# Second chunk's first ternary ahead of the minimum over the lags, and both row sums behind the next group's first copy, in an octonion FFN kernel with a lag bound

## The chip, the cores and the metric

The kernel runs on one core of a Trainium2 chip. The metric is device time in microseconds; three runs of the kernel before gave 606.47, 607.83 and 608.39, so the median is 607.83. A core has a matrix engine, TensorE (PE in the profile, its weight loads PEld), and three engines for elementwise work: VectorE (DVE), ScalarE (ACT) and GpSimd (POOL). SyncE (SP) issues the DMAs. Each engine takes its instructions in the order in which they are written and waits on semaphores that the others raise; an instruction that waits holds up everything behind it on its engine.

## The reference

The input x has 2048 rows of 1024 values. Each row is normalised, and two branches are added to x: an attention over time lags, and a feed-forward net whose weights are ternary and multiplied as octonions.

```python
x = L0_attn_x
xn = _layernorm(x, axis=-1)
x = x + _L0_attn_ref(xn) + _L0_ffn_ref(xn, w_gate, w_up, w_down)

# attention: circular autocorrelation by FFT, softmax over the 6 largest lags, weighted sum of rolled rows
f = jnp.fft.rfft(xh, axis=-1)
corr = jnp.fft.irfft(f * jnp.conj(f), n=L, axis=-1)
weights, delay = jax.lax.top_k(corr, top_k)

# feed-forward: every weight tensor W (8, out/8, in/8) is made ternary with one threshold
scale = jnp.mean(jnp.abs(W))
Wq = scale * jnp.clip(jnp.round(W / scale), -1.0, 1.0)
M = jnp.einsum('jik,jod->koid', S_OCT, Wq)      # S_OCT: the signed table of octonion products
out = jnp.einsum('...id,koid->...ko', xp, M)
# h = silu(gate(x)) * up(x), then down(h);  w_gate, w_up: (8, 341, 128), w_down: (8, 128, 341)
```

For these inputs the lag at zero dominates the softmax so far that the attention branch is the normalised row itself. The kernel proves that row by row with a bound (it needs the smallest value over the lags of a short transform) and only takes a slow path where the bound fails.

## The kernel before

The 2048 rows are taken in 8 groups of 256 rows, each of two tiles of 128. The 341 hidden values of each octonion part are split into three chunks c of 114, 114 and 113. The work is a list of units, and each unit owns one of four pairs of accumulator banks, `acc`:

- T(m,c): transposes of the weights of matrix m (0 gate, 1 up, 2 down), chunk c. ACT then takes signs (L636), DVE turns them ternary in place of the sign (`ternary`, L906), and DVE builds sums and differences of weight blocks from them (`weight_slots`, L923 to L931).
- X(g,i): transposes of half of the normalised x of group g (L419), split by ACT and DVE in a high and a low 16-bit part.
- G(g,c,Y) and U(g,c,Y): gate and up products of chunk c, output half Y. After the spectral part (L375) ACT copies two of the four quarters to `pk` (`odd_two`, L681), DVE adds and subtracts (`first_adds` L980 to L984, `second_adds` L1014 to L1028), and PE adds the terms (L382). For G, ACT applies SiLU (L707 to L710); for U, DVE multiplies into `hx` (`product`, L1077). In group 0 the first two chunks are computed directly (L402).
- For each product, POOL forms half sums (L1313 to L1319), and ACT and POOL round the product (ACT L725, POOL L1321) and the sums (ACT L736, POOL L1324) into the 16-bit operand `hop` of the down product.
- N(g,t): the down product of one tile (L479), scaled and added to the output tile by DVE (L1172).
- F(g): a transform of the folded x (L432), its power by ACT (L695), and the lag matmuls (L440). DVE then takes the minimum over the lags (`least`, L1082).

The layer norm of group g is made while group g-1 runs: ACT sums each of the two tiles (`row_sum`, L585, and the mean at L588), then their squares (`row_var`, L599); POOL makes 1/sqrt by one power and one Newton step (`rstd`, L1270 to L1283), ACT normalises (L604), and DVE multiplies the halves of each row (`dot`, L939). After that the unit X of group g can be transposed.

What comes after what is written out. The opening (weights and group 0) is a list for each engine. The steady part is one loop over the places n of the unit list, in which every engine has its own dictionaries of what to add at which place. PE makes the spectral part of unit n and then the terms of unit n-2. A group begins with G(b,0,0), U(b,0,0), and the unit ahead of it is F(b). Before a unit begins, PE waits until the unit that owned its banks before has been read (`take_banks`).

Of the kernel before, what the change touches and what calls it, by code (L numbers as in the profile page):

```python
def octonion_ffn_attention_kernel(nc, x, w_gate, w_up, w_down, dft, lag, out):
# [15 lines left out]
    G = ROWS // T  # L17
# [70 lines left out]
    place = {u: n for n, u in enumerate(units)}  # L88
# [36 lines left out]
    sum_at, var_at, rstd_at, norm_at, dot_at = {}, {}, {}, {}, {}  # L125
    for g in range(2, G):
        a, b = g - 2, g - 1
        sum_at[place["F", b]], sum_at[place["G", b, 0, 0]] = (g, 0), (g, 1)
        var_at[place["U", b, 0, 0]], var_at[place["G", b, 0, 1]] = (g, 0), (g, 1)
        rstd_at[u_no["U", b, 0, 0]] = g  # L130
        norm_at[place["N", b - 1, 0]] = g
# [14 lines left out]
    for u in u_no:  # L146
        _, g, c, Y = u
# [11 lines left out]
    with ctx:  # L159
# [414 lines left out]
        def _(act):  # L574
# [5 lines left out]
            def row_sum(g, t):  # L580
                k = NT * g + t
                act.wait_ge(x_in[t], 16 * (g + 1))
                act.wait_ge(sum_done, k - 1)
                act.wait_ge(var_done, NT * g)
                nc.scalar.activation(junk[:, :], xr[:, t, :], ACT.Copy, accum_out=sm[:, k:k + 1]).then_inc(sum_done, 1)  # L585
                if t == NT - 1:
                    act.wait_ge(sum_done, k)
                    nc.scalar.activation(nm[:, NT * g:NT * g + NT], sm[:, NT * g:NT * g + NT], ACT.Copy, scale=-1.0 / D).then_inc(mean_done, 1)  # L588
# [12 lines left out]
            def normalise(g, t):  # L601
                k = NT * g + t
                act.wait_ge(ln_done, g + 1)
                nc.scalar.activation(xr[:, t, :], xr[:, t, :], ACT.Identity, bias=nmrs[:, k:k + 1], scale=rs[:, k:k + 1]).then_inc(norm_done, 1)  # L604
# [78 lines left out]
            def x_high(u):  # L683
                act.wait_ge(x_mm, x_no[u] + 1)
                nc.scalar.activation(xop[:, u[1] % 2, 4 * u[2]:4 * u[2] + 4, 0, :], bank_pair(place[u]).rearrange("p b (i t) -> p (b i) t", t=T),
                                     ACT.Copy, scale=XS).then_inc(xhi_done, 1)
# [6 lines left out]
            def power(u):  # L693
                act.wait_ge(dft_mm, f_no[u] + 1)
                nc.scalar.activation(pw[:, :, :].rearrange("p m t -> p (m t)"), acc[:, bank[place[u]], 0, :], ACT.Square, scale=POWER).then_inc(power_done, 1)  # L695
# [16 lines left out]
            def h_high(u):  # L712
                _, g, c, Y = u
                m = u_no[u]
                h = hx[0:CH, m % 4, :, :]
                if m == 0:
                    act.wait_ge(abs_done[2], 1)
                if m < LAST:
                    act.wait_ge(h_done, m + 1)
                else:  # L720
                    act.wait_ge(tail_pair, 2)
                    h = last_h
                for v in free_after[g, c]:
                    act.wait_ge(term_mm, prod_no[v] + 1)
                nc.scalar.activation(half_of(g, c, 4 * Y, 0), by_tile(h), ACT.Copy).then_inc(hhi_done, 1)  # L725

            def h_sums_high(u):
                _, g, c, Y = u
                m = u_no[u]
                if m < LAST:  # L730
                    act.wait_ge(hs_done, 2 * m + 2)
                    sums = hs[:, 0:4, :]
                else:
                    act.wait_ge(tail_sum, 2)
                    sums = last_sums
                nc.scalar.activation(half_of(g, c, NJ + 4 * Y, 0), by_tile(sums), ACT.Copy).then_inc(hhs_done if m < LAST else tail_high, 1)  # L736
# [64 lines left out]
            for n in range(OPEN, N + 8):  # L801
                if n in norm_at:
                    normalise(norm_at[n], 0)
                    normalise(norm_at[n], 1)
                if n in z_at:
                    g, t = z_at[n]
                    k = NT * g + t
                    act.wait_ge(zx_in[t], 16 * (g + 1))
                    nc.scalar.activation(zx[:, t, :], zx[:, t, :], ACT.Identity, bias=nmrs[:, k:k + 1], scale=onep[:, k:k + 1]).then_inc(z_done, 1)
                if n in round_at:  # L810
                    h_sums_high(round_at[n])
                if n in high_at:
                    h_high(high_at[n])
                if 2 <= n < N and units[n - 2] == ("U", G - 1, NC - 1, 1):

                    for b in range(2):
                        act.wait_ge(tail_mult, b + 1)
                        nc.scalar.activation(hx[0:CH, LAST % 4, 2 * b + 1, :], last_h[:, 2 * b + 1, :], ACT.Copy).then_inc(tail_odd, 1)
                if n < N:
                    u = units[n]  # L820
                    if u[0] in "GUNX":
                        odd_two(u)
                    if u[0] == "X":
                        x_high(u)
                    if u[0] == "F":
                        power(u)
                if n in x_sums:
                    x_sums_high(x_sums[n])
                if n in silu_at:
                    silu(silu_at[n])  # L830
                if n == OPEN + 1:
                    eights(("T", 1, 1))
                if n in sum_at:
                    row_sum(*sum_at[n])
                if n in var_at:
                    row_var(*var_at[n])

# [18 lines left out]
        def _(dve):  # L856
# [43 lines left out]
            def ternary(u):  # L900
                _, m, c = u
                k, n = t_no[u], place[u]
                rows, cols, val = weights_of(u)
                for b in range(2):
                    dve.wait_ge(sign_done, 2 * k + b + 1)
                    nc.vector.scalar_tensor_tensor(val[:, 4 * b:4 * b + 4, :],  # L906
                                                   acc[0:rows, bank[n], b, :].rearrange("p (j d) -> p j d", j=4)[:, :, 0:cols],
                                                   thr[0:rows, m:m + 1], wt[k % 2][0:rows, 4 * b:4 * b + 4, 0:cols], ALU.is_gt, ALU.min).then_inc(tern_done, 1)

            def weight_slots(u):  # L910
                _, m, c = u
                i = slots_no[u]
                rows, cols, val = weights_of(u)
                dve.wait_ge(tern_done, 2 * t_no[u] + 2)
                two = val.rearrange("p (b i v) d -> p b i v d", b=2, i=2)
                s = tt[i % 2][0:rows, :, :, 0:cols]
                if u == ("T", 1, 0):

                    dve.wait_ge(first_slots, 1)
                if u == ("T", 2, 2):  # L920

                    dve.wait_ge(term_mm, prod_no["G", 0, 1, 1] + 1)
                nc.vector.tensor_tensor(s[:, 0:3:2, :, :], two[:, :, 0, :, :], two[:, :, 1, :, :], ALU.add)  # L923
                nc.vector.tensor_tensor(s[:, 1:4:2, :, :], two[:, :, 0, :, :], two[:, :, 1, :, :], ALU.subtract).then_inc(pairs_done, 1)
                dve.wait_ge(pairs_done, i + 1)
                for op, (a, alu) in enumerate(((0, ALU.add), (0, ALU.subtract), (1, ALU.add), (1, ALU.subtract))):
                    if m < 2:
                        dst = (wg, wu)[m][:, c, 4 * op:4 * op + 4, 0:cols].rearrange("p (b v) d -> p b v d", b=2)
                    else:
                        dst = wd[0:rows, 4 * op:4 * op + 4, c, :].rearrange("p (b v) d -> p b v d", b=2)  # L930
                    last = nc.vector.tensor_tensor(dst, s[:, a:a + 1, :, :].broadcast_to([rows, 2, 2, cols]), s[:, 2:4, :, :], alu)  # L931
                last.then_inc(slots_done, 1)
# [147 lines left out]
            def least(u):  # L1080
                dve.wait_ge(lag_mm, f_no[u] + 1)
                nc.vector.tensor_reduce(dmin[:, NT * u[1]:NT * u[1] + NT], acc[:, bank[place[u]], 1, :].rearrange("p (t l) -> p t l", t=NT),  # L1082
                                        AX.X, ALU.min).then_inc(bound_done, 1)
# [30 lines left out]
            weight_slots(("T", 1, 2))  # L1114

            product(("U", 0, 0, 0))
            least(("F", 0))
            ternary(("T", 0, 1))
            weight_slots(("T", 0, 1))
            ternary(("T", 1, 1))  # L1120
            thresholds(2, ("T", 1, 1))
            product(("U", 0, 0, 1))
# [20 lines left out]
            for n in range(OPEN, N + 2):  # L1143
# [19 lines left out]
                if n >= OPEN + 2:  # L1163
                    v = units[n - 2]
                    if v[0] == "N":
                        _, g, t = v
# [193 lines left out]
```

## Time and profile before

| | before |
|---|---|
| median of 3 runs | 607.83 us (606.47 to 608.39) |
| the profiled execution, time | 607.72 us |
| the profiled execution, span | 605.7 us |
| PE busy | 583.6 us, 96% |
| weight loads (PEld) | 543.0 us, 90% |
| DVE busy | 508.4 us, 84% |
| POOL busy | 462.8 us, 76% |
| ACT busy | 354.7 us, 59% |

The span is that of one profiled execution, and its own time lies 2.0 us above it. PE's matmuls overlap and their ends are modelled, so 96% busy doesn't mean that the array is never kept waiting for a weight load; but the gaps that the profile does show are short and few. Busy shares of the other engines say little by themselves: what counts is which of them PE waits for at a given place.

### The profile page before, as it was taken

The numbers are of one execution on the slowest core, as the hardware profiler recorded it, in microseconds if no ns is written. First come the engines' busy times: TensorE is split into PE (matmuls) and PEld (weight loads), VectorE is DVE, ScalarE is ACT, GpSimd is POOL, SyncE is SP. The second block draws the span as 40 slices with busy tenths as digits, with TensorE's granted clock in tenths as the row PEclk, the third lists the DMA queues.
The fourth block names the chain that finished last, engine by engine and source line by source line (L and its number), as shares of the span: only waits on it lengthen the run. The fifth ranks groups of instructions, "written<-read, shape, count | busy, mean of one in ns | idle before, by whom it ended". The sixth has DMA issues, their size and how long they took to land.

```text
span 605.7 us, 16440 instructions
## 1 busy us (share of the span) xinstructions
PE 583.6 (96%) x6764; PEld 543.0 (90%) x6764; DVE 508.4 (84%) x1230; ACT 354.7 (59%) x497; POOL 462.8 (76%) x362
## 2 busy tenths in 40 slices
PE   7998999979999999999999999999999999999996
PEld 7998998869989998899989998899989998998896
DVE  4886898879898989989888989989898989967854
ACT  4677967664567635774476545774576645543540
POOL 3415749998769977999769977999679977987920
PEclk9999999999999999999999999999999999999999
DMA  9720011001040023002040013002030101002011
GB/s 208 158 71 1 1 71 71 2 1 70 3 140 2 4 71 119 22 2 70 3 140 2 37 37 141 1 2 72 1 140 2 42 32 70 2 3 70 1 71 72
DMA packets 10251, 30.67 MB, mean 51 GB/s; under 512 B 928, under 2 KB 4032, under 8 KB 10176
## 3 DMA queue, kind: packets, MB, share of 16 engines
q1 hardware_dynamic: 10176, 29.62, 15.3%
q8 instruction: 53, 0.87, 0.6%
q14 instruction: 22, 0.18, 0.1%
HBM read 21.23 MB, written 8.39 MB: 49 GB/s over the span
## 4 chain that ended last, share of the span: by engine, by line
POOL 54%; issue 30%; PE 14%; DVE 1%; POOLq 0%; ACT 0%; ACTq 0%
POOL hop L1324 16%; POOL hs L1318 10%; POOL hs L1319 10%; POOL hs L1314 9%; POOL hs L1313 6%; PE acc L479 5%; PE acc L402 4%; PE acc L411 2%; PE acc L382 1%; POOL r L1272 1%; POOL hop L1321 1%; PE acc L456 1%; PE acc L375 0%; POOL hop L1254 0%; PE acc L419 0%
## 5 line engine op out<-in xcount | busy, mean ns | idle before, releaser
L479 PE MATMUL acc<-wd,hop 114*128 114x128 f16 (+1 forms) x2944 | 171.4, 220 | 1.0 <-POOL hop L1324 0.7
L479 PEld LDWEIGHTS acc<-wd,hop 114*128 114x128 f16 (+1 forms) x2944 | 168.3, 98 | 2.2 <-POOL hop L1324 0.9
L681 ACT ACTIVATE pk<-acc 114x512 f32<-114x512 f32 (+1 forms) x120 | 70.7, 589 | 71.6 <-PE acc L479 34.1
L1313 POOL TENSOR_TENSOR hs<-hx 114x512 f32<-114x512 f32 x47 | 60.3, 1282 | 68.4 <-DVE hx L1077 60.4
L1324 POOL TENSOR_TENSOR hop<-hs,hop 114x1024 f16<-114x1024 f32 x46 | 98.2, 2135 | 7.9 <-ACT hop L736 7.9
L1321 POOL TENSOR_TENSOR hop<-hx,hop 114x1024 f16<-114x1024 f32 x46 | 98.3, 2138 | 0.6 <-ACT hop L725 0.6
L382 PE MATMUL acc<-xop,wg 128*128 128x256 f16 x704 | 84.1, 273 | 4.5 <-DVE acc L1028 4.4
L725 ACT ACTIVATE hop<-hx 114x1024 f16<-114x1024 f32 x46 | 48.6, 1057 | 65.4 <-DVE hx L1077 65.4
L375 PE MATMUL acc<-xop,wg 128*128 128x256 f16 x704 | 84.2, 273 | 1.0 <-DVE hx L1077 0.9
L382 PE MATMUL acc<-xop,wu 128*128 128x256 f16 x704 | 84.1, 273 | 0.7
L375 PE MATMUL acc<-xop,wu 128*128 128x256 f16 x704 | 84.1, 273 | 0.7 <-DVE hx L1077 0.7
L980 DVE TENSOR_TENSOR bd<-acc,pk 114x256 f32<-114x256 f32 (+1 forms) x104 | 43.7, 421 | 48.2 <-ACT pk L681 48.0
L382 PEld LDWEIGHTS acc<-xop,wg 128*128 128x128 f16 x704 | 68.3, 98 | 14.2 <-DVE acc L1028 6.0
L375 PEld LDWEIGHTS acc<-xop,wu 128*128 128x128 f16 x704 | 68.7, 98 | 9.2 <-DVE hx L1077 1.0
L375 PEld LDWEIGHTS acc<-xop,wg 128*128 128x128 f16 x704 | 67.7, 98 | 10.2 <-DVE hx L1077 2.6
L382 PEld LDWEIGHTS acc<-xop,wu 128*128 128x128 f16 x704 | 67.8, 98 | 10.0 <-DVE acc L1028 2.3
L736 ACT ACTIVATE hop<-hs 114x1024 f16<-114x1024 f32 x46 | 48.6, 1057 | 45.6 <-POOL hs L1319 45.4
L1318 POOL TENSOR_TENSOR hs<-hs 114x512 f32<-114x512 f32 x47 | 62.4, 1328 | 3.7
L1319 POOL TENSOR_TENSOR hs<-hs 114x512 f32<-114x512 f32 x47 | 62.5, 1331 | 0.0
L1077 DVE SCALAR_TENSOR_TENSOR hx<-hx,few,acc 114x1024 f32<-114x1024 f32 x47 | 59.8, 1272 | 1.8 <-PE acc L402 1.8
L1314 POOL TENSOR_TENSOR hs<-hx 114x512 f32<-114x512 f32 x47 | 60.2, 1280 | 0.0
L984 DVE TENSOR_TENSOR acc<-acc,pk 114x256 f32<-114x256 f32 (+1 forms) x104 | 44.0, 423 | 0.0
(164 smaller groups left out, 929.3 us busy)
## 6 DMA issues: line engine op xcount, KB each, us to landing
xr<-in_x SPq DMA_DIRECT2D x16, 512.0 KB, 4.8
zx<-in_x SPq DMA_DIRECT2D x16, 512.0 KB, 4.0
out_y<-zx SPq DMA_DIRECT2D x16, 512.0 KB, 3.0
hop<-in_w_down SPq DMA_DIRECT2D x1, 1364.0 KB, 19.3
hop<-in_w_gate SPq DMA_DIRECT2D x2, 576.0 KB, 9.5
hop<-in_w_up SPq DMA_DIRECT2D x1, 1152.0 KB
hop<-in_w_gate SPq DMA_DIRECT2D x1, 192.0 KB
hop<-in_w_up SPq DMA_DIRECT2D x1, 192.0 KB
```

Source lines behind the costliest of these rows:

```text
L375: last = nc.tensor.matmul(acc[:, bank[n], s // 2, T * (s % 2):T * (s % 2 + 1)], wm[:, c, slot, :], xop[:, g % 2, form, level, :], start=s ...
L382: last = nc.tensor.matmul(acc[:, bank[n], s // 2, T * (s % 2):T * (s % 2 + 1)], wm[:, c, slot, :], xop[:, g % 2, form, level, :], start=Fa ...
L479: last = nc.tensor.matmul(acc[:, bank[n], s // 2, at:at + P], operand(g, c, t, form, level), wd[0:WIDE[c], slot, c, :], start=which == 0 a ...
L681: nc.scalar.activation(pk[0:rows, q % 2, :, :], pair[:, :, T:2 * T], ACT.Copy, scale=XS if u[0] == "X" else 1.0).then_inc(copied, 1)
L725: nc.scalar.activation(half_of(g, c, 4 * Y, 0), by_tile(h), ACT.Copy).then_inc(hhi_done, 1)
L1077: nc.vector.scalar_tensor_tensor(hx[0:CH, m % 4, :, :], hx[0:CH, m % 4, :, :], scale[0:CH, :], bank_pair(place[u], CH).rearrange("p b (i t ...
L1313: nc.gpsimd.tensor_tensor(hs[:, 4:8:2, :], h[:, 0:4:2, :], h[:, 1:4:2, :], ALU.add)
L1314: nc.gpsimd.tensor_tensor(hs[:, 5:8:2, :], h[:, 0:4:2, :], h[:, 1:4:2, :], ALU.subtract).then_inc(hpair_done, 1)
L1318: nc.gpsimd.tensor_tensor(hs[:, 0:2, :], hs[:, 4:6, :], hs[:, 6:8, :], ALU.add).then_inc(hs_done, 1)
L1319: nc.gpsimd.tensor_tensor(hs[:, 2:4, :], hs[:, 4:6, :], hs[:, 6:8, :], ALU.subtract).then_inc(hs_done, 1)
L1321: nc.gpsimd.tensor_tensor(half_of(g, c, 4 * Y, 1), by_tile(h), half_of(g, c, 4 * Y, 0), ALU.subtract).then_inc(h_free, 1)
L1324: nc.gpsimd.tensor_tensor(half_of(g, c, NJ + 4 * Y, 1), by_tile(hs[:, 0:4, :]), half_of(g, c, NJ + 4 * Y, 0), ALU.subtract).then_inc(h_rea ...
```

## The change

Two places are written in another order; no instruction is added or removed.

```diff
-        sum_at[place["F", b]], sum_at[place["G", b, 0, 0]] = (g, 0), (g, 1)
+        sum_at[place["G", b, 0, 0]] = g
...
                 if n in sum_at:
-                    row_sum(*sum_at[n])
+                    row_sum(sum_at[n], 0)
+                    row_sum(sum_at[n], 1)
...
             product(("U", 0, 0, 0))
-            least(("F", 0))
             ternary(("T", 0, 1))
             weight_slots(("T", 0, 1))
+            least(("F", 0))
             ternary(("T", 1, 1))
```

The code after is one line longer ahead of VectorE's part, so its lines there have numbers higher by one (L906 becomes L907, L1324 becomes L1325); ScalarE's keep theirs up to L834.

VectorE, opening, before: the product of U(0,0,0) (L1077), the minimum over the lags of F(0) (L1082, `dmin`), the ternary of T(0,1) (L906 on `wg`), its sums (L923 to L931), and the ternary of T(1,1) (L906 on `wu`).

```order
L1077 SCALAR_TENSOR_TENSOR hx<-hx,few,acc 114x1024
L1082 TENSOR_REDUCE dmin<-acc 128x2
L906 SCALAR_TENSOR_TENSOR wg<-acc,few,zx 128x4x114 x2
L923 TENSOR_TENSOR zx<-wg 128x2x2x114
L924 TENSOR_TENSOR zx<-wg 128x2x2x114
L931 TENSOR_TENSOR wg<-zx 128x4x114 x4
L906 SCALAR_TENSOR_TENSOR wu<-acc,few,zx 128x4x114 x2
```

VectorE, the same place, after the change (line numbers one higher).

```order
L1078 SCALAR_TENSOR_TENSOR hx<-hx,few,acc 114x1024
L907 SCALAR_TENSOR_TENSOR wg<-acc,few,zx 128x4x114 x2
L924 TENSOR_TENSOR zx<-wg 128x2x2x114
L925 TENSOR_TENSOR zx<-wg 128x2x2x114
L932 TENSOR_TENSOR wg<-zx 128x4x114 x4
L1083 TENSOR_REDUCE dmin<-acc 128x2
L907 SCALAR_TENSOR_TENSOR wu<-acc,few,zx 128x4x114 x2
```

The minimum has moved behind eight instructions, the ternary of T(0,1) and its sums; nothing else on VectorE differs.

ScalarE at the start of group 2, before: the power of F(2) (L695), SiLU of the last gate unit of group 1 (L710), a row sum, the copy of G(2,0,0) to `pk` (L681), the other row sum and the mean, and then rounding of the half sums (L736) and of the product (L725).

```order
L695 ACTIVATE pw<-acc 128x512 [waits dft_mm]
L710 ACTIVATE hx<-acc,few 114x1024 [waits h_free,term_mm]
L585 ACTIVATE junk,sm<-xr 128x1024 [waits var_done,sum_done,x_in0]
L681 ACTIVATE pk<-acc 114x512 [waits spec_mm,l1_done]
L585 ACTIVATE junk,sm<-xr 128x1024 [waits var_done,sum_done,x_in1]
L588 ACTIVATE nm<-sm 128x2 [waits sum_done]
L736 ACTIVATE hop<-hs 114x2x4x128 [waits hs_done]
L725 ACTIVATE hop<-hx 114x2x4x128 [waits term_mm,h_done]
```

ScalarE, the same place, after the change.

```order
L695 ACTIVATE pw<-acc 128x512 [waits dft_mm]
L710 ACTIVATE hx<-acc,few 114x1024 [waits h_free,term_mm]
L681 ACTIVATE pk<-acc 114x512 [waits spec_mm,l1_done]
L585 ACTIVATE junk,sm<-xr 128x1024 [waits var_done,sum_done,x_in0]
L585 ACTIVATE junk,sm<-xr 128x1024 [waits var_done,sum_done,x_in1]
L588 ACTIVATE nm<-sm 128x2 [waits sum_done]
L736 ACTIVATE hop<-hs 114x2x4x128 [waits hs_done]
L725 ACTIVATE hop<-hx 114x2x4x128 [waits term_mm,h_done]
```

The copy has moved ahead of the first row sum, and the two row sums now stand one behind the other. The same happens at the start of groups 1 to 6; group 1 differs in that L725 alone stands behind the mean, and the rounding of the sums follows later. Queues of TensorE, GpSimd and SyncE are the same as before.

## Rows read from the trace of the kernel before

**Rows 1.** The waits of TensorE (PE): us in total, times, longest us.
```profile
PE acc L382 <- DVE acc L1028: 4.4, 6, 0.7
...
PE acc L419 <- DVE hx L1077: 2.8, 1, 2.8
```

**Rows 2.** Timeline, PE, opening: start us, duration us, instruction [idle before <-releaser].
```profile
47.98 0.60 PE L440 MATMUL acc<-lag_sb,pw 128*128 128x256 f16 x4
50.56 1.00 PE L456 MATMUL acc<-ident,hop 114*128 114x114 f32 x8 [1.98 <-DVE wg L906]
...
55.07 1.04 PE L419 MATMUL acc<-ident,xr 128*128 128x128 f32 x8
...
59.44 1.04 PE L456 MATMUL acc<-ident,hop 128*114 128x128 f32 x8
```

**Rows 3.** Timeline, VectorE (DVE), same place.
```profile
48.62 0.69 DVE L1082 TENSOR_REDUCE dmin<-acc 128x2 f32<-128x512 f32 x1 [3.87 <-PE acc L440]
49.23 1.28 DVE L906 SCALAR_TENSOR_TENSOR wg<-acc,few,zx 128x456 f16<-128x456 f32 x2
```

**Rows 4.** Timeline, ScalarE (ACT), opening.
```profile
37.76 1.06 ACT L585 ACTIVATE junk<-xr 128x1024 f16<-128x1024 f32 x1
...
38.99 1.06 ACT L585 ACTIVATE junk<-xr 128x1024 f16<-128x1024 f32 x1
...
44.69 1.17 ACT L636 ACTIVATE zx<-acc,few 128x456 f16<-128x456 f32 x2 [0.19 <-PE acc L456]
...
48.21 2.36 ACT L604 ACTIVATE xr<-xr,nmrs,rs 128x1024 f32<-128x1024 f32 x2
```

**Rows 5.** Timeline, ACT, first pair of row sums moved (start of group 1).
```profile
103.41 1.06 ACT L585 ACTIVATE junk<-xr 128x1024 f16<-128x1024 f32 x1
...
104.45 0.59 ACT L681 ACTIVATE pk<-acc 114x512 f32<-114x512 f32 x1
```

**Rows 6.** Timeline, DVE, same place.
```profile
106.41 1.27 DVE L1077 SCALAR_TENSOR_TENSOR hx<-hx,few,acc 114x1024 f32<-114x1024 f32 x1
```

**Rows 7.** Timeline, PE, group 1.
```profile
107.74 1.92 PE L375 MATMUL acc<-xop,wg 128*128 128x256 f16 x16 [0.89 <-DVE hx L1077]
...
122.84 1.96 PE L479 MATMUL acc<-wd,hop 113*128 113x128 f16 x32 [0.74 <-POOL hop L1324]
...
134.14 7.16 PE L479 MATMUL acc<-wd,hop 114*128 114x128 f16 x96 [0.24 <-DVE acc L1002]
```

**Rows 8.** Timeline, GpSimd (POOL), group 1.
```profile
111.41 2.14 POOL L1324 TENSOR_TENSOR hop<-hs,hop 114x1024 f16<-114x1024 f32 x1 [0.54 <-ACT hop L736]
```

**Rows 9.** Timeline, ACT, group 2.
```profile
177.44 0.58 ACT L681 ACTIVATE pk<-acc 114x512 f32<-114x512 f32 x1
177.92 1.05 ACT L585 ACTIVATE junk<-xr 128x1024 f16<-128x1024 f32 x1
...
179.20 1.04 ACT L736 ACTIVATE hop<-hs 114x1024 f16<-114x1024 f32 x1
...
194.34 2.37 ACT L604 ACTIVATE xr<-xr,nmrs,rs 128x1024 f32<-128x1024 f32 x2 [0.98 <-POOL onep L1283]
```

**Rows 10.** Timeline, POOL, group 2.
```profile
180.32 2.13 POOL L1324 TENSOR_TENSOR hop<-hs,hop 114x1024 f16<-114x1024 f32 x1 [1.03 <-ACT hop L736]
```

**Rows 11.** Timeline, DVE, group 2.
```profile
200.38 1.27 DVE L1077 SCALAR_TENSOR_TENSOR hx<-hx,few,acc 114x1024 f32<-114x1024 f32 x1
...
202.56 0.42 DVE L1002 TENSOR_TENSOR acc<-acc,bd 128x256 f32<-128x256 f32 x1
```

**Rows 12.** Timeline, PE, group 2.
```profile
175.19 1.91 PE L375 MATMUL acc<-xop,wg 128*128 128x256 f16 x16
...
202.24 1.04 PE L419 MATMUL acc<-ident,xr 128*128 128x128 f32 x8
203.11 5.53 PE L479 MATMUL acc<-wd,hop 114*128 114x128 f16 x96
```

**Rows 13.** Windows: stretch, us, busy of PE, PEld, DVE, ACT, POOL; granted clock; DMA.
```profile
134.00:136.00 2.00, 1.86 (x20) 1.86 (x21) 1.73 (x6) 2.00 (x5) 2.00 (x2) 0.60 0.00 0
```

## The prediction, written before the changed kernel was run

> **What bounds the kernel now.** I read the list of TensorE's waits first, because TensorE (PE) has almost no idle time: the reader is to see that only a few short waits are left, and that every one is ended by an instruction of DVE or POOL [rows 1]. The largest family, six waits of 0.7 us behind DVE L1028, lies at the end of each group, before the row sums start; it is a loop of PE, ACT and DVE over the last unit of the group, and the change moves nothing in it. Two others belong to the change: the wait of 1.98 us behind DVE L906 at 50.56 in the opening [rows 2], and 0.89 us behind DVE L1077 at 107.74 [rows 7]. Next I read the timeline of each engine round those two places, and last round the same place one group later, since the row sums come back six times (g from 2 to 7, beside groups 1 to 6) and a wait that is absent today may appear there. Groups 2 to 6 repeat one pattern, so rows of group 2 stand for five.
>
> **The opening.** Today DVE reaches the minimum over the lags early and stands for 3.87 us until the lag matmuls are done; only then come the two instructions of the ternary T(0,1), at 49.23 for 1.28 us [rows 3]. PE, which finished those lag matmuls at 48.58, needs the bank of T(0,1) for the transposes of T(1,1) and waits 1.98 us, until 50.56 [rows 2]. The signs that the ternary needs are ready at 44.69 + 1.17 = 45.86 [rows 4]. With the ternary first, its second half can start at about 45.9 and be done at 46.6, which is 2 us before PE asks for the bank. So the wait goes, and nothing on DVE takes its place: the sums of T(0,1) (6 instructions) fill the time in which DVE stood idle, and the minimum starts about when it does today. Since ends of overlapping matmuls are modelled (four take 0.60, but PE issues one every (1.91 - 0.27)/15 = 0.11 us by a row of 16 [rows 12], taking 0.27 for one), PE could go on as early as 47.98 + 0.44 = 48.42. That bounds the gain by 1.98 and 2.14 us; I take 2.1.
>
> What is late next? The normalisation on ACT ends at 48.21 + 2.36 = 50.57 [rows 4]; its reader, the transposes of X(1,0), stands at 55.07 [rows 2] and would stand at 53.0. The signs of T(1,1) follow the normalisation at 50.5, their ternary is done by 52.5, and their bank is asked for by T(2,0) at 59.44 today [rows 2], 57.3 then. POOL starts its first product earlier, but it later stands waiting for a DVE product anyway, so that buys nothing and costs nothing. From there to the end of the opening PE is busy without a wait, and what feeds it is fed by it, so I let the 2.1 us through in full.
>
> **Row sums, group 1.** The first sum now stands between SiLU and the copy `pk`: it starts at 103.41, the copy at 104.45 [rows 5]. With the copy first, DVE's quad and then its product come 1.04 us earlier than 106.41 [rows 6], and PE's unit at 107.74, which waits for that product's end at 107.68 (so a released engine starts 0.06 us later), comes at 106.7: the 0.89 us are gone [rows 7]. But the next wait is POOL's: PE stands 0.74 us at 122.84 for POOL's last rounding [rows 7], and POOL was held up only 0.54 us by ACT [rows 8]. ACT is ahead there by 1.04, so POOL gains those 0.54 and no more. PE arrives a full 1.04 earlier and waits longer. Gain of this group: 0.55 us.
>
> **Row sums, groups 2 to 6.** Here PE's spectral unit ends at 175.19 + 1.91 = 177.10 [rows 12], and the copy starts at 177.44, just behind the first row sum. So the copy can gain at most about 0.25 us (177.2 instead of 177.44). The price is on ACT behind it. Today the first sum fits into the time in which ACT would wait for PE. Then it follows the copy: first sum at 177.2 + 0.48 (the step from the copy to the next instruction today, [rows 9]) = 177.68. Two row sums in a row are also not 1.04 apart but 38.99 - 37.76 = 1.23 us [rows 4], because the second waits for the first one's accumulator to be read: second sum at 178.91. Today it starts at 177.92, and the rounding of the half sums, L736, at 179.20 [rows 9], 1.28 later. So L736 moves to 180.19, later by 0.99 us. This is the queue behind the moved instruction, and POOL waits for its head: POOL L1324 already waits 1.03 us for exactly L736 [rows 10].
>
> From there I follow the 1.0 us. POOL works through that unit, the next one and then the Newton steps of the layer norm, with no idle between; ACT's normalisation at 194.34 has waited 0.98 us for POOL, so it follows in full [rows 9]. DVE's two dots wait for the normalisation; behind them on DVE's queue stand the quad of the unit N, the product at 200.38 and the second sums, whose last ends at 202.56 + 0.42 = 202.98 [rows 11]. PE needs these at 202.24 (transposes; the product ends at 201.65, slack 0.59 less the 0.06) and at 203.11 (terms of N; slack 0.13 less 0.06 = 0.07) [rows 12]. Slack 0.07 against a delay of 0.99: PE loses 0.92 us in each such group. Up to 1.0 is possible if a later unit leans on the same DVE queue without slack. The delay is not given back before the group ends, since there PE sets the pace; and POOL's backlog is gone by then, so the five do not pile up. Five times 0.92 to 1.0 is 4.6 to 5.0; I take 4.8. Below: were the pair 1.04 apart, the delay would be 0.80 and the sum 5 x 0.73 = 3.7; were DVE to find a way round, nothing.
>
> **Sum.** -2.1 - 0.55 + 4.8 = +2.15 us on the profiled execution's 607.72, so 609.9. Its own time is 0.1 us below the median of the runs shown (607.83), so I leave it there.
>
> **A place where the clock speaks.** TensorE was idle 2.76 us before the transposes of group 1 (the 2.8 of [rows 1]); behind that, the granted clock averages 0.60 over 134 to 136 us, a mix of 2.4 and 1.2 GHz [rows 13], and 96 matmuls take 7.16 instead of 5.53 us [rows 7, 12], a loss of 1.63. The Trainium skill, page "TensorE: Matmul & The Clock Gate", section "Why this matters for your kernels", warns that idle gaps between bursts bring TensorE back to half rate. By that rule the trace agrees, and it speaks for the same loss after, because the 2.76 us behind POOL's chain stay: the order of the products there is unchanged.
>
> **Rivals.**
> (a) *The delay never reaches PE.* If DVE or ACT has more slack than I read, only the gains stand: 607.72 - 2.65 = 605.1, faster by 0.4%. For it: POOL and ACT are far from full over the span and wait in other places. Against: 0.98 and 1.03 us of idle on the chain itself, both ended by its predecessor, say that the chain is tight. Chance 0.15.
> (b) *Only part of it comes through*, 0.3 to 0.7 us a group (the second sum does not wait 1.23, or the product's earlier start shifts DVE's queue): 606.6 to 608.6, middle 607.9. Chance 0.18.
> (c) *The opening gives nothing*: PE's 2.1 us turn into a wait at X(1,0) or at the end of the opening, while groups 2 to 6 cost 4.8: 612.0, slower. For it: ACT and DVE are dense up to 90 us; against: PE is never idle between 51 and 106 us and both queues hang on PE. Chance 0.10.
> (d) *The clock.* The slow stretch does not come, 608.3, or comes a second time since PE's idle in group 1 is 0.5 us longer in sum, 611.5. Chance 0.07, half each.
> My forecast has 0.50. A kernel of this length is told from no change at about 0.3%, 1.8 us. Faster is (a), 0.15. Within 0.3% are (b), half of (d) and a quarter of the forecast's own spread: 0.18 + 0.03 + 0.12 = 0.33. Slower is the rest, 0.52. The forecast's own range is 608.8 to 611.0; the one that holds 8 in 10 reaches from 606.2 to 612.1.
>
> **What would show it.** In the opening: no PE wait behind DVE L907 (L906 moved by one line), DVE's minimum behind the sums. Group 1: the 0.89 gone, the wait for POOL grown from 0.74 to about 1.2. Groups 2 to 6: ACT's rounding about 1.0 later behind the copy, POOL L1325 waiting 2.0 instead of 1.0, and new PE waits at the transposes of X (0.4) and at N's terms (0.5) that add up to 0.9 five times, with each of these groups longer by that. If their length stays, (a) holds and I am wrong in sign; if the two PE waits are there but small, (b).

## The result, and the profile after

| | before | after |
|---|---|---|
| median | 608.19 us (9 runs, 606.47 to 609.35) | 609.78 us (9 runs, 608.79 to 610.44) |
| ratio | | 1.0037, 95% interval 1.0027 to 1.0047 |
| the profiled execution, time and span | 607.72 and 605.7 us | 609.15 and 607.1 us |
| PE busy | 583.6 us | 585.6 us |
| POOL busy | 462.8 us | 462.9 us |

The changed kernel is slower by 0.37%, about 2.2 us by the ratio. The forecast was 609.9 us, with slower as the likeliest outcome.

TensorE's waits in the profile after (us in total, times, longest):

```profile
PE acc L382 <- DVE acc L1029: 4.4, 6, 0.7
...
PE acc L419 <- DVE hx L1078: 3.2, 4, 2.8
PE acc L479 <- DVE acc L1003: 1.2, 5, 0.2
PE acc L479 <- POOL hop L1325: 1.2, 1, 1.2
```

The wait behind the ternary (DVE L906 before, L907 now) has left the list. In its stead the transposes of X wait four times instead of once, the terms of N five times instead of once, and the wait for POOL has grown from 0.74 to 1.18 us. The six waits of 0.7 at the ends of groups are the ones of [rows 1].

The opening, TensorE and then VectorE (columns as in [rows 2]):

```profile
47.81 0.60 PE L440 MATMUL acc<-lag_sb,pw 128*128 128x256 f16 x4
48.25 0.94 PE L456 MATMUL acc<-ident,hop 114*128 114x114 f32 x8
```

```profile
45.19 1.29 DVE L907 SCALAR_TENSOR_TENSOR wg<-acc,few,zx 128x456 f16<-128x456 f32 x2 [0.61 <-ACT zx L636]
...
48.49 0.68 DVE L1083 TENSOR_REDUCE dmin<-acc 128x2 f32<-128x512 f32 x1
```

The transposes of T(1,1) follow the lag matmuls at once, 0.44 us after their start, where they came 2.58 us after it in [rows 2]. The ternary of T(0,1) is over at 46.5, and the minimum starts at 48.49, which in [rows 3] was 48.62: VectorE's idle time really was filled.

Group 1, TensorE and POOL:

```profile
104.34 1.92 PE L375 MATMUL acc<-xop,wg 128*128 128x256 f16 x16
...
119.88 1.96 PE L479 MATMUL acc<-wd,hop 113*128 113x128 f16 x32 [1.18 <-POOL hop L1325]
...
129.83 1.93 PE L419 MATMUL acc<-ident,xr 128*128 128x128 f32 x8 [2.75 <-DVE hx L1078]
131.56 6.37 PE L479 MATMUL acc<-wd,hop 114*128 114x128 f16 x96
```

```profile
108.47 2.13 POOL L1325 TENSOR_TENSOR hop<-hs,hop 114x1024 f16<-114x1024 f32 x1
```

The wait of 0.89 us at G(1,0,1) ([rows 7]) is gone, and POOL L1325 no longer waits for ScalarE as it did in [rows 8]. TensorE now stands longer for POOL at 119.88, and then as long as before, 2.75 us, at the transposes of X. The slow stretch of the clock is here again, in another place: it covers the transposes (1.93 us for 8) and part of the terms of N (6.37 us for 96, where it was 7.16 in [rows 7]).

Group 2, ScalarE, POOL, VectorE and TensorE, the rows that answer to [rows 9 to 12]:

```profile
173.81 0.60 ACT L681 ACTIVATE pk<-acc 114x512 f32<-114x512 f32 x1 [0.69 <-PE acc L375]
174.31 1.05 ACT L585 ACTIVATE junk<-xr 128x1024 f16<-128x1024 f32 x1
...
175.53 1.06 ACT L585 ACTIVATE junk<-xr 128x1024 f16<-128x1024 f32 x1
...
176.82 1.04 ACT L736 ACTIVATE hop<-hs 114x1024 f16<-114x1024 f32 x1
...
191.95 2.37 ACT L604 ACTIVATE xr<-xr,nmrs,rs 128x1024 f32<-128x1024 f32 x2 [1.55 <-POOL onep L1284]
```

```profile
177.94 2.13 POOL L1325 TENSOR_TENSOR hop<-hs,hop 114x1024 f16<-114x1024 f32 x1 [2.02 <-ACT hop L736]
```

```profile
197.99 1.26 DVE L1078 SCALAR_TENSOR_TENSOR hx<-hx,few,acc 114x1024 f32<-114x1024 f32 x1
```

```profile
170.05 1.92 PE L382 MATMUL acc<-xop,wg 128*128 128x256 f16 x16 [0.72 <-DVE acc L1029]
...
199.31 1.09 PE L419 MATMUL acc<-ident,xr 128*128 128x128 f32 x8
200.65 5.53 PE L479 MATMUL acc<-wd,hop 114*128 114x128 f16 x96 [0.25 <-DVE acc L1003]
...
238.34 1.92 PE L382 MATMUL acc<-xop,wg 128*128 128x256 f16 x16 [0.72 <-DVE acc L1029]
...
511.53 1.92 PE L382 MATMUL acc<-xop,wg 128*128 128x256 f16 x16 [0.73 <-DVE acc L1029]
```

The rows of the kernel before that are counted from, at X's transposes of group 1 and at the first terms of groups 2 and 7:

```profile
132.80 1.09 PE L419 MATMUL acc<-ident,xr 128*128 128x128 f32 x8 [2.76 <-DVE hx L1077]
...
173.43 1.92 PE L382 MATMUL acc<-xop,wg 128*128 128x256 f16 x16 [0.73 <-DVE acc L1028]
...
510.09 1.92 PE L382 MATMUL acc<-xop,wg 128*128 128x256 f16 x16 [0.73 <-DVE acc L1028]
```

To compare with before, count from the start of the group's first terms, L382, at 173.43 before and 170.05 after. The rounding L736 came 5.77 us behind it and now comes 6.77; POOL L1324/L1325 6.89 and 7.89; the normalisation 20.91 and 21.90; VectorE's product 26.95 and 27.94; the transposes of X 28.81 and 29.26; N's terms 29.68 and 30.60. So ScalarE's 1.0 us arrives at VectorE whole, and 0.92 of it at TensorE. From group to group TensorE's L382 is 68.29 us apart (238.34 - 170.05); before, the mean of the five periods from 173.43 to 510.09 is 67.33. This distance is called the period below. Five such groups are 4.8 us.

### The profile page after: what moved, and what is told of

It is laid out like the page before. It is cut to its first block, busy times and chain, and to the rows that moved or that the text cites. A ratio compares the mean times of both kernels' runs of the same rounds, so it can differ in the third digit from the quotient of the medians.

```text
span 607.1 us, 16440 instructions
## 1 busy us (share of the span) xinstructions
PE 585.6 (96%) x6764; PEld 541.6 (89%) x6764; DVE 508.3 (84%) x1230; ACT 354.9 (58%) x497; POOL 462.9 (76%) x362
## 4 chain that ended last, share of the span: by engine, by line
POOL 53%; issue 31%; PE 11%; DMA 2%; DVE 1%; SPq 0%; ACT 0%; POOLq 0%; ACTq 0%
POOL hop L1325 15%; POOL hs L1319 10%; POOL hs L1320 10%; POOL hs L1315 9%; POOL hs L1314 6%; PE acc L479 5%; PE acc L402 4%; DMA hop<-in_w_gate 2%; PE acc L382 1%; POOL r L1273 1%; POOL hop L1322 1%; PE acc L456 1%; PE acc L375 0%; PE acc L419 0%; PE acc L411 0%
## 5 line engine op out<-in xcount | busy, mean ns | idle before, releaser
L681 ACT ACTIVATE pk<-acc 114x512 f32<-114x512 f32 (+1 forms) x120 | 70.5, 588 | 71.2 <-PE acc L375 37.1
L1325 POOL TENSOR_TENSOR hop<-hs,hop 114x1024 f16<-114x1024 f32 x46 | 98.1, 2133 | 12.8 <-ACT hop L736 12.8
L382 PE MATMUL acc<-xop,wg 128*128 128x256 f16 x704 | 84.1, 273 | 4.5 <-DVE acc L1029 4.4
L382 PE MATMUL acc<-xop,wu 128*128 128x256 f16 x704 | 84.1, 273 | 0.7
L725 ACT ACTIVATE hop<-hx 114x1024 f16<-114x1024 f32 x46 | 48.5, 1055 | 59.4 <-DVE hx L1078 59.4
L382 PEld LDWEIGHTS acc<-xop,wg 128*128 128x128 f16 x704 | 68.3, 98 | 14.2 <-DVE acc L1029 6.0
L736 ACT ACTIVATE hop<-hs 114x1024 f16<-114x1024 f32 x46 | 48.6, 1056 | 53.1 <-POOL hs L1320 53.1
L382 PEld LDWEIGHTS acc<-xop,wu 128*128 128x128 f16 x704 | 67.8, 98 | 9.9 <-DVE acc L1029 2.4
```

Of the source, the lines that this page charges most:

```text
L382: last = nc.tensor.matmul(acc[:, bank[n], s // 2, T * (s % 2):T * (s % 2 + 1)], wm[:, c, slot, :], xop[:, g % 2, form, level, :], start=Fa ...
L681: nc.scalar.activation(pk[0:rows, q % 2, :, :], pair[:, :, T:2 * T], ACT.Copy, scale=XS if u[0] == "X" else 1.0).then_inc(copied, 1)
L1325: nc.gpsimd.tensor_tensor(half_of(g, c, NJ + 4 * Y, 1), by_tile(hs[:, 0:4, :]), half_of(g, c, NJ + 4 * Y, 0), ALU.subtract).then_inc(h_rea ...
```

## The experiments

All ran beside runs of the kernel before (median 607.73 us beside the first four, 607.71 beside the last three). Each was written to move one term of the sum or to cut the chain at one place.

**Opening only.** VectorE's order in the opening is changed, ScalarE's is that of before.

```diff
-            least(("F", 0))
             ternary(("T", 0, 1))
             weight_slots(("T", 0, 1))
+            least(("F", 0))
```

> Only the opening's reorder on VectorE (ternary and sums of T(0,1) ahead of the minimum), row sums as before. My theory: the three terms are independent, so this one alone takes 2.1 us off: ratio 0.9965, about 606.1 against 608.2, and TensorE's wait behind the ternary at 50.6 is gone while every later wait of before (0.89, 0.74, 2.76, six of 0.73) is still there. Rival A, the opening's gain is given back later in the opening or at POOL's wait in group 1: ratio 1.000. Rival B, the opening is where the change loses: above 1.002.

Measured: 604.88 us, ratio 0.9951 (0.9939 to 0.9964). TensorE:

```profile
48.38 0.94 PE L456 MATMUL acc<-ident,hop 114*128 114x114 f32 x8
...
105.51 1.92 PE L375 MATMUL acc<-xop,wg 128*128 128x256 f16 x16 [0.89 <-DVE hx L1077]
...
120.59 1.96 PE L479 MATMUL acc<-wd,hop 113*128 113x128 f16 x32 [0.73 <-POOL hop L1324]
...
130.55 1.69 PE L419 MATMUL acc<-ident,xr 128*128 128x128 f32 x8 [2.76 <-DVE hx L1077]
```

The waits of 0.89, 0.74 and 2.76 us are still there, so the gain is the opening's and is passed on whole: T(1,1) starts 2.18 us earlier than in [rows 2], the unit behind the 0.89 us 2.23 us earlier than in [rows 7]. Rivals A and B fall. The timed gain, 2.85 us by the medians, is 0.7 larger than I had expected; 0.4 of it, in the profiled execution, is the slow stretch, which in this profile starts at the transposes and in the one of before in N's terms (from X's transposes to the next group's L382 are 40.22 us here, 40.63 in the profile of before). The rest is within the interval.

**Row sums only.** The opening is that of before, the row sums are those of the changed kernel.

```diff
-        sum_at[place["F", b]], sum_at[place["G", b, 0, 0]] = (g, 0), (g, 1)
+        sum_at[place["G", b, 0, 0]] = g
```

> Only the row sums' reorder on ScalarE, opening as before. My theory: -0.6 in group 1 and +0.96 in each of groups 2 to 6, +4.2 in all: ratio 1.0070, about 612.4. TensorE's new waits stand at the transposes of X and the terms of N, and the rounding L736 comes 1.0 later. Rival: the reorder is neutral by itself and only costs together with the opening (ratio 1.000); or the loss is in one place only (ratio 1.000 to 1.003).

Measured: 612.02 us, ratio 1.0075 (1.006 to 1.009). TensorE's waits:

```profile
PE acc L419 <- DVE hx L1078: 3.6, 6, 2.8
...
PE acc L456 <- DVE wg L907: 2.0, 1, 2.0
PE acc L479 <- DVE acc L1003: 1.5, 6, 0.2
```

The opening's wait is back, and the waits at X and N are there, six of each where the changed kernel has four and five. The period is 68.32 us, as in the changed kernel. The profiled execution took 611.0 us, 1.0 less than the median: it has no slow stretch of the clock, and the six runs spread from 610.7 to 613.4. The two halves of the change add up: 0.9951 x 1.0075 = 1.0026, with the interval of the whole (1.0027 to 1.0047) inside what the intervals of the two allow. The rival that the halves need one another falls.

**Row sums moved in group 1 only**, with the opening's reorder.

```diff
+        if g == 2:
+            sum_at[place["G", b, 0, 0]] = ((g, 0), (g, 1))
+        else:
+            sum_at[place["F", b]], sum_at[place["G", b, 0, 0]] = ((g, 0),), ((g, 1),)
```

> Opening's reorder, and the row sums moved behind the copy only at the start of group 1; groups 2 to 6 as before. My theory: -2.1 and -0.6 without the cost: ratio 0.9955, about 605.5, faster than both kernels. In groups 2 to 6 the pattern of before comes back: L736 waited for 1.03 us by POOL, period 67.33. Rival, the loss of the changed kernel came from group 1 or from the phase in which the groups start: the period stays at 68.3 and the ratio is 1.002 or more.

Measured: 604.65 us, ratio 0.9950 (0.9938 to 0.9962): faster than both kernels. POOL and TensorE in group 2:

```profile
176.95 2.13 POOL L1328 TENSOR_TENSOR hop<-hs,hop 114x1024 f16<-114x1024 f32 x1 [1.03 <-ACT hop L739]
```

```profile
170.05 1.92 PE L385 MATMUL acc<-xop,wg 128*128 128x256 f16 x16 [0.72 <-DVE acc L1032]
...
237.39 1.92 PE L385 MATMUL acc<-xop,wg 128*128 128x256 f16 x16 [0.73 <-DVE acc L1032]
```

TensorE at X's transposes of group 1:

```profile
129.78 1.39 PE L422 MATMUL acc<-ident,xr 128*128 128x128 f32 x8 [2.77 <-DVE hx L1081]
```

POOL waits 1.03 us for the rounding, as before, and the group takes 67.34 us: the loss was in groups 2 to 6, and not in the phase that the opening hands on. What the move is worth in group 1 the times can't tell (604.65 against 604.88, each uncertain by 0.7). The traces show it: X's transposes start 0.77 us earlier than in the kernel with the opening alone (129.78 and 130.55). In this kernel the opening's T(1,1) already starts 0.22 us earlier (48.16 and 48.38), so the move in group 1 is worth 0.55 us.

**The dots taken off the chain.** The changed kernel, with VectorE's two dots one unit N later.

```diff
+        dot_at[place["N", b - 1, 1]] = g
...
-                if n in norm_at and kind == "N":
-                    dot(norm_at[n], 0)
-                    dot(norm_at[n], 1)
+                if n in dot_at:
+                    dot(dot_at[n], 0)
+                    dot(dot_at[n], 1)
```

> The changed kernel with one thing more: VectorE's two dots of the normalised rows (L939) no longer stand ahead of the quad of N(b-1,0) but ahead of that of N(b-1,1), where VectorE idles 2 us. They are what ties the product and N's sums to POOL's Newton steps and ScalarE's normalisation. My theory: ScalarE's rounding is still 1.0 late and POOL still waits 2.0 for it, but it reaches TensorE no more: the 0.96 us of each of groups 2 to 6 vanish (-4.8), and the 2.76 us of idle in group 1 shrinks to about 1 (-1.8): ratio to before about 0.992, 603.2. Rival, the delay reaches TensorE by another way (POOL's rounding of the operands for N, or the banks): the period stays near 68.3 and only group 1 gains, ratio about 1.000.

Measured: 603.26 us, ratio 0.9927 (0.9915 to 0.9939). POOL and TensorE:

```profile
175.73 2.13 POOL L1326 TENSOR_TENSOR hop<-hs,hop 114x1024 f16<-114x1024 f32 x1 [2.03 <-ACT hop L737]
```

```profile
127.90 1.09 PE L420 MATMUL acc<-ident,xr 128*128 128x128 f32 x8 [0.94 <-DVE hx L1079]
...
167.84 1.92 PE L383 MATMUL acc<-xop,wg 128*128 128x256 f16 x16 [0.73 <-DVE acc L1030]
...
177.31 1.91 PE L383 MATMUL acc<-xop,wg 128*128 128x256 f16 x16
179.18 1.92 PE L376 MATMUL acc<-xop,wu 128*128 128x256 f16 x16
...
235.31 1.92 PE L383 MATMUL acc<-xop,wg 128*128 128x256 f16 x16 [0.72 <-DVE acc L1030]
```

This is the sharpest of the tests: POOL still waits 2.03 us for the late rounding, exactly as in the changed kernel, but no wait is left at X or N in groups 2 to 6, and the period falls from 68.29 to 67.47. So 0.82 of the 0.96 us reached TensorE through the normalisation and the dots. What is left over before's 67.33 is 0.14 us a group: the unit U(g,0,1) starts 1.87 us after the terms ahead of it, not 1.74 as in the kernel before (177.31 and 179.18). It takes the banks of F(g), which the minimum over the lags reads:

```profile
178.45 0.68 DVE L1084 TENSOR_REDUCE dmin<-acc 128x2 f32<-128x512 f32 x1
```

The minimum ends at 179.13, 0.05 us before the unit starts, and it is late because VectorE ahead of it waits 0.92 us for ScalarE's next copy to `pk`, which stands behind the two row sums (0.27 us in the kernel with the opening alone). In group 1 the wait at X shrinks from 2.76 to 0.94, and a new one of 0.85 appears at 140.86, 13 us farther on. The time of 603.3 was forecast as 603.2, but partly by luck. Of the 1.8 us forecast for group 1, 0.9 was lost again at that new wait, and the five groups gave back 4.15 us (five times 0.83) and not 4.8. The slow stretch of the clock, 1.2 us in the profile of the changed kernel, is absent from this one, and that was not in the forecast.

**The second row sum one unit later**, the copy still ahead of the first, with the opening's reorder.

```diff
-        sum_at[place["F", b]], sum_at[place["G", b, 0, 0]] = (g, 0), (g, 1)
+        sum_at[place["G", b, 0, 0]], sum_at[place["U", b, 0, 0]] = (g, 0), (g, 1)
```

> Opening's reorder; the copy ahead of the first row sum as in the changed kernel, but the second row sum and the mean one unit later, behind the two roundings L736 and L725 and the next copy. My theory (the cost is what stands ahead of L736, not that the copy goes first): in groups 2 to 6 L736 comes 0.5 us earlier than before, POOL waits about 0.5 for it, TensorE gets no new wait and the period is 67.33. In group 1 the second sum now stands ahead of the rounding that POOL waits for, so 0.3 us are lost there: about 605.2 against 608.0, ratio 0.9955. Rival (the copy ahead of the sum, or the longer wait of the layer norm for its mean, costs by itself): a period of 67.6 or more and a ratio of 0.998 or more.

Measured: 605.46 us, ratio 0.9958 (0.9943 to 0.9973). ScalarE, POOL and TensorE:

```profile
176.14 1.04 ACT L736 ACTIVATE hop<-hs 114x1024 f16<-114x1024 f32 x1
```

```profile
177.26 2.13 POOL L1324 TENSOR_TENSOR hop<-hs,hop 114x1024 f16<-114x1024 f32 x1 [0.56 <-ACT hop L736]
```

```profile
120.79 1.96 PE L479 MATMUL acc<-wd,hop 113*128 113x128 f16 x32 [1.80 <-POOL hop L1324]
...
170.84 1.92 PE L382 MATMUL acc<-xop,wg 128*128 128x256 f16 x16 [0.72 <-DVE acc L1028]
...
238.17 1.92 PE L382 MATMUL acc<-xop,wg 128*128 128x256 f16 x16 [0.72 <-DVE acc L1028]
```

The copy first does no harm: with one row sum ahead of L736 the rounding comes 5.30 us behind L382 (5.77 before, 6.77 after), POOL waits 0.56, and the period is 67.33. In group 1 TensorE now stands 1.80 us for POOL, since there the second sum has come ahead of the rounding; that is the loss that was expected. So the place of the copy is not the cause; the work ahead of L736 is.

**A little more work ahead of L736**, in the kernel before, with nothing moved. The added copy writes a scratch result.

```diff
                     row_sum(*sum_at[n])
+                    g, t = sum_at[n]
+                    if g > 2 and t == 1:
+                        act.wait_ge(sum_done, NT * g + 1)
+                        nc.scalar.activation(junk[:, 0:D // 4], xr[:, 1, 0:D // 4], ACT.Copy).then_inc(extra_done, 1)
+                        act.wait_ge(extra_done, g - 2)
```

> The kernel before, with one small copy more on ScalarE (128 x 256 elements, a scratch result that nobody reads) between the mean and L736 at the start of groups 2 to 6. Nothing else is moved. My theory: L736 comes later by the 0.4 to 0.5 us that it takes, and TensorE loses all of that but the slack of 0.07, five times: period 67.7 to 67.8, +1.7 to +2.2 us, ratio 1.003 to 1.0035. Rival (there is more slack than 0.07 us, and the changed kernel lost its time because of the order and not the delay): period 67.33 and ratio 1.000.

Measured: 609.81 us, ratio 1.0037 (1.0023 to 1.0051). ScalarE, POOL and TensorE:

```profile
178.81 0.40 ACT L838 ACTIVATE junk<-xr 128x256 f16<-128x256 f32 x1
179.24 1.06 ACT L736 ACTIVATE hop<-hs 114x1024 f16<-114x1024 f32 x1
```

```profile
180.38 2.13 POOL L1329 TENSOR_TENSOR hop<-hs,hop 114x1024 f16<-114x1024 f32 x1 [1.48 <-ACT hop L736]
```

```profile
173.04 1.92 PE L382 MATMUL acc<-xop,wg 128*128 128x256 f16 x16 [0.73 <-DVE acc L1033]
...
203.09 5.54 PE L479 MATMUL acc<-wd,hop 114*128 114x128 f16 x96 [0.21 <-DVE acc L1007]
...
240.78 1.92 PE L382 MATMUL acc<-xop,wg 128*128 128x256 f16 x16 [0.72 <-DVE acc L1033]
```

L736 stands 6.20 us behind L382, 0.43 later than before; POOL waits 1.48 instead of 1.03, and the period is 67.74, longer by 0.41. At the terms of N TensorE is 0.37 us late (203.09 - 173.04 against 203.11 - 173.43), where it was 0.92 late for a delay of 1.00. That is a slack of 0.06 to 0.08, as read from [rows 11, 12]. The other 0.04 us are lost farther on in the group, in both kernels, where a later gate unit starts 1.85 us (changed) and 1.84 us (this one) behind the unit ahead of it, and 1.80 before. So 0.43 us of delay cost 0.41 us, and 1.00 us cost 0.96.

**The best of them.** The opening, the row sums moved in group 1 only, and the dots later; the edits are those of the two kernels above.

> Opening's reorder, row sums behind the copy in group 1 only, and VectorE's dots one unit N later. My theory: the last kernel with later dots (603.3) still had a period of 67.47, since ScalarE's later copies made the minimum over the lags late for the unit U(g,0,1); with the sums of groups 2 to 6 where they were, the period is 67.33 and 5 x 0.14 = 0.7 us go: 602.6, ratio 0.9912. Rival (the 0.14 come from the dots' new place): period 67.47 and 603.3.

Measured: 602.61 us, ratio 0.9909 (0.9891 to 0.9927). TensorE:

```profile
128.70 1.09 PE L423 MATMUL acc<-ident,xr 128*128 128x128 f32 x8 [0.95 <-DVE hx L1082]
...
168.66 1.92 PE L386 MATMUL acc<-xop,wg 128*128 128x256 f16 x16 [0.72 <-DVE acc L1033]
...
235.98 1.92 PE L386 MATMUL acc<-xop,wg 128*128 128x256 f16 x16 [0.72 <-DVE acc L1033]
```

The period is 67.32, so the later dots by themselves change no period, and the 0.14 belonged to the doubled row sums and not to the dots. This kernel is faster than the one before by 0.9% and than the changed one by some 1.3%.

## Why the prediction was right, point by point

- *The opening, -2.1.* Right in mechanism; size 2.2 in the traces (the lag matmuls of group 1, L440, start at 106.25 before and at 103.88 after, 2.37 earlier, of which 0.17 are an earlier start of the whole). The minimum took nothing, the normalisation was not late (TensorE's X(1,0) came without a wait), and nothing in the opening gave the time back. The kernel with the opening alone shows it by itself.
- *Group 1, -0.55.* The reasoning was that ScalarE gains 1.04 us, that TensorE takes it at once, and that POOL's chain allows only 0.54 of it. In the trace the 0.89 us are gone, the wait for POOL is 1.18 where about 1.2 was forecast, and TensorE leaves it 2.96 us earlier than before, of which 2.4 are the opening's and an earlier start's. That leaves 0.6 for this group, and 0.55 between the kernel with group 1 only and the one with the opening alone. Shown in traces; too small for the times.
- *Groups 2 to 6, +4.8.* Every link of the chain came out within 0.02 us: second row sum 1.22 us behind the first (forecast 1.23), L736 1.00 later (0.99), POOL 1.00, normalisation 0.99, TensorE 0.92 at N's terms and 0.96 at the group's end (0.92 to 1.0). The dots' kernel cuts the chain and 0.82 of the 0.96 us go; the added copy, put into the kernel before, delays the same chain by 0.43 us and costs 0.41.
- *The sum.* In the profiled execution: -0.17 for an earlier start, -2.20 opening, -0.60 group 1, -0.41 for the slow stretch, +4.82 for five groups (511.53 - 170.05 against 510.09 - 173.43), in all +1.44; 607.72 + 1.44 = 609.16, and the profiled time is 609.15. The forecast had +2.15. Of the 0.7 us between, 0.6 are the earlier start and the cheaper stretch, neither of which it had. By the times the change costs 1.6 to 2.9 us, which holds the forecast and just misses the 1.4 of this one pair of executions.
- *What I had wrong.* The waits at X and N (0.4 and 0.5): the profile prints 0.16 or nothing and 0.25. Part of that is the view: printed idle counts from a modelled end of the matmuls before, which overlaps the next start when nothing waits, so starts have to be compared. X starts 0.45 us later and N's terms 0.92. But I also didn't see the minimum's bank: 0.12 us at U(2,0,1), which stands at 181.39, 1.87 behind the terms ahead of it. With 0.02 more by the next units it is 0.14 of X's 0.45, so the step into X itself grew by 0.31 only, and the one from X to N's terms by 0.47. In the changed kernel the 0.14 cost nothing, since TensorE would have waited for VectorE at X and N anyway; they count in the kernel with the later dots.
- *The rivals.* (a), the delay hidden: fell by the period, which grew. (b), only part of it: fell by the same, since it grew by 0.96. (c), the opening gives nothing: fell by the first experiment. (d), the clock: the stretch was there again in the profiled execution, once, at another place, and cost 0.4 less. That it was there was forecast; that it cost less was not.

## What to carry to other kernels

An idle gap of an engine ahead of an instruction is free room only for as much work as fits in it: here the first row sum stood in ScalarE's wait for TensorE, and moved out of it, it cost about its full length (1.04 us long, 1.00 us of delay) at the next instruction that another engine was waiting for. Before moving work behind an urgent instruction, look at what is now behind the work, and follow that one across engines until it meets either an idle gap larger than the delay or the bound engine. And where one edit is made at a place that repeats, read a later repetition and not the first: in group 1 this move gained, in the five after it lost.

## What the runs showed of the hardware

- Two row sums (activations with an accumulator) that wait for one another start 1.22 to 1.24 us apart, against 1.04 from a row sum to an unrelated copy. In the profile of before the copy at 177.44 starts 0.09 us after the reading of the accumulator has begun (177.35). In the profile after, the second row sum at 175.53 starts 0.28 us after it (175.25): it waits until that reading, 0.19 us, is over.
- The slow stretch of TensorE's clock, at 1.2 GHz, appeared behind the 2.8 us of idle in group 1 in five of the seven profiles that have that idle (before, after, opening only, group 1 only, second sum later), and in neither of the two in which it is 0.95 us. The same 2.8 us are without it in two (row sums only, added copy). The kernel with the added copy has such a stretch in the opening instead, behind its wait of 1.98 us. From X's transposes to the next L382 are 39.02 us without the stretch (row sums only) and 40.08 to 40.63 with it, so it costs 1.1 to 1.6 us.
- The record has a mean granted clock for every run, over the whole span, and for the kernel before it goes with the time. Of its 29 runs beside the experiments, 5 have 0.999 (606.4 to 606.7 us), 16 have 0.996 or 0.997 (607.4 to 607.9), and 8 have 0.992 to 0.994 (608.2 to 609.9). So one and the same kernel has more or less of the slow clock from run to run, and most of its spread of 3.5 us goes with that. Of the 12 runs of the two kernels with later dots, whose idle in group 1 is 0.95 us, one has 0.997 and the others 0.998 to 1.0; in the kernel before 24 of 29 have 0.997 or less. The mean also takes in the last microseconds, in which TensorE has no work left and the clock falls too, so it can't be turned into a count of stretches. That the shorter idle is what spares those kernels the stretch is likely and not shown, since no run changes that idle alone.
